# Expert low parts on VectorE, and two output adds per tile instead of one

## The reference

```python
def moe(x, gate_w, expert_w, expert_b):          # _L0_ffn_ref
    xf = x.reshape(B * S, D)
    gate_logits = xf @ gate_w.T
    top_vals, top_idx = jax.lax.top_k(gate_logits, 2)
    w = jax.nn.softmax(top_vals, axis=-1)
    y_all = einsum('td,eod->teo', xf, expert_w) + expert_b[None]
    y_sel = take_along_axis(y_all, top_idx[:, :, None], axis=1)
    return sum(y_sel * w[:, :, None], axis=1)
x = x + attention(layernorm(x), Wq, bq, Wk, bk, Wv, bv, Wo, bo)
x = x + moe(layernorm(x), gate_w, expert_w, expert_b)
```

## Time and profile before

| | |
|---|---|
| median of 3 runs | 1817.34 us (1815.02 to 1827.36) |
| the profiled execution | 1809.88 us, span 1808.1 us |
| TensorE (PE) busy | 1653.4 us, 91% |
| VectorE (DVE) busy | 1432.6 us, 79% |
| ScalarE (ACT) busy | 1272.3 us, 70% |
| GpSimd (POOL) busy | 538.6 us, 30% |

### The profile page before, as it was taken

How to read it: one execution, slowest core, us unless ns; L and a number is a source line. 1 busy time by engine, 2 the same in 40 slices (tenths; PEclk the granted TensorE clock), 3 DMA queues, 4 the chain that set the end, 5 groups by cost and what they waited for, 6 DMA issues and landing times.

```text
span 1808.1 us, 38316 instructions
## 1 busy us (share of the span) xinstructions
PE 1653.4 (91%) x13754; PEld 806.7 (45%) x13755; DVE 1432.6 (79%) x1619; ACT 1272.3 (70%) x2387; POOL 538.6 (30%) x735
## 2 busy tenths in 40 slices
PE   5999999999999999999999999999999987677762
PEld 3533444444444444444444444444444355556551
DVE  3288999999999999999999999999999137653331
ACT  2325888888888888888888888888888953322221
POOL 3111222222233322223223322222224464342222
PEclk9998999999999999999999999999999998688996
DMA  6346422432332243224222332223211433565441
GB/s 195 88 116 138 71 72 58 103 70 58 75 82 60 63 105 82 58 72 102 58 58 60 84 85 64 81 65 67 58 34 37 134 131 134 200 137 99 85 84 20
DMA packets 78946, 155.68 MB, mean 86 GB/s; under 512 B 19504, under 2 KB 23616, under 8 KB 78048
## 3 DMA queue, kind: packets, MB, share of 16 engines
q1 hardware_dynamic: 41776, 72.20, 17.8%
q0 software_dynamic: 34592, 79.71, 16.7%
q10 hardware_dynamic: 2448, 1.84, 0.5%
HBM read 76.38 MB, written 77.67 MB: 85 GB/s over the span
## 4 chain that ended last, share of the span: by engine, by line
PE 79%; DMA 12%; issue 4%; DVE 3%; ACT 1%; ACTq 1%; POOL 1%; SPq 0%; DVEq 0%; POOLq 0%; another core or an unknown queue 0%
PE bank L911 32%; PE bank L872 24%; PE bank L901 16%; DMA out_y<-ys,tok_i 10%; PE bank L844 3%; PE bank L992 1%; DVE max_kc L1166 1%; PE bank L859 1%; DMA x_all<-in_L_attn_x 1%; DMA q_st<-q_parts 0%; DMA arena_p<-in_L_attn_bv 0%; ACTq L662 0%; ACT we_hi L745 0%; PE bank L882 0%; POOL x_all L464 0%
## 5 line engine op out<-in xcount | busy, mean ns | idle before, releaser
L1166 DVE TENSOR_REDUCE max_kc<-bank 128x1 f32<-128x1024 f32 x1024 | 1241.2, 1222 | 75.3 <-PE bank L872 55.3
L735 ACT ACTIVATE arena_p<-bank 128x512 f32<-128x512 f32 x2048 | 1108.7, 596 | 163.4 <-PE bank L901 131.4
L911 PE MATMUL bank<-arena_p,v_cur 128*32 128x256 f32 x8192 | 655.7, 392 | 5.7 <-issue 5.7
L872 PE MATMUL bank<-k_st,q_st 48*128 48x512 f32 x2048 | 511.7, 497 | 5.5 <-DMA q_st<-q_parts 4.2
L901 PE MATMUL bank<-q_st,k_st 50*128 50x512 f32 x2048 | 447.7, 409 | 0.3 <-ACT arena_p L735 0.3
L872 PEld LDWEIGHTS bank<-k_st,q_st 48*128 48x128 f32 x2048 | 191.0, 183 | 430.3 <-issue 384.0
L901 PEld LDWEIGHTS bank<-q_st,k_st 50*128 50x128 f32 x2048 | 298.1, 185 | 35.4 <-ACT arena_p L735 22.4
L911 PEld LDWEIGHTS bank<-arena_p,v_cur 128*32 128x32 f32 x8192 | 162.6, 108 | 292.8 <-issue 149.2
L428 POOL DMA_DIRECT2D sums<-o_acc x128 | 65.3, 516 | 395.9 <-ACT o_acc L715 395.7
L806 ACT ACTIVATE ys<-bank,gate 128x512 f32<-128x512 f32 x39 | 26.8, 687 | 157.8 <-DMA out_y<-ys,tok_i 131.9
L1385 DVE SCALAR_TENSOR_TENSOR ys<-x_all,gate,ys 128x512 f32<-128x512 f32 x39 | 29.3, 751 | 122.9 <-ACT ys L806 120.2
(11 more groups left out here) (161 smaller groups left out, 924.2 us busy)
## 6 DMA issues: line engine op xcount, KB each, us to landing
slots_x<-pad_row POOLq DMA_DIRECT2D x27, 1290.0 KB, 5.8
q_st<-q_parts SPq DMA_DIRECT2D x192, 128.0 KB, 4.6
xs<-slots_x SPq DMA_DIRECT2D x39, 258.0 KB
q_parts<-parts SPq DMA_DIRECT2D x16, 512.0 KB, 3.7
we_raw<-in_L_ffn_expert_w POOLq DMA_DIRECT2D x8, 1024.0 KB, 7.9
at_parts<-o_hl POOLq DMA_DIRECT2D x128, 64.0 KB, 2.3
k_st<-k_parts SPq DMA_DIRECT2D x48, 128.0 KB, 4.8
rec_b<-sums_rec POOLq DMA_DIRECT2D x128, 32.0 KB, 1.9
```

Source lines behind the costliest of these rows:

```text
L735: act.activation(probs[:, u % PRING, :], bank[:, ring_bank(("score", u)), :], ACT.Exp, scale=SCALE).then_inc(p_ready, 1)
L872: return pe.matmul(bank[:, 2 + 2 * (m % 2) + q, :], q_st[r:r + CROW, j % SLOTS, h, qt * P:(qt + 1) * P], k_st[r:r + CROW, key_slot(j // NC ...
L911: mm = pe.matmul(bank[32 * h:32 * h + 32, 6, half], v_cur[:, kt, :], probs[:, (REP * kt + h) % PRING, half], start=(kt == 0 and part == 0) ...
L1166: dve.reduce_max(max_kc[:, m:m + 1], bank[:, 2 + 2 * (m % 2):4 + 2 * (m % 2), :].rearrange("p a s -> p (a s)"), AX.X).then_inc(m_done, 1)
```

## The change

It has two parts. (a) The low parts of experts 0 to 4 are formed on VectorE, each behind the `scaling` of tiles 2, 3, 5, 6 and 9; ScalarE's high part of expert 3 moves from tile 6 to tile 5. (b) Every tile s gets two indirect adds. `add_tile(s, 0)` ("now") is issued with tile s and has the tile's row numbers if the tile ahead has the same expert; otherwise 4096 is added to all of them, so that every row is dropped. `add_tile(s, 1)` ("later") is issued one tile later, behind the "now" add of tile s+1, and has the real numbers exactly where "now" has not. Two tiles of one expert hold no token in common. Before its two adds, step s waits until all "now" adds up to s-2 and all "later" adds up to s-2 have landed; the "now" add of s-1 may be in flight. The flags (`away`) are made with the lists of experts, three small operations in `list_out`, which runs twice.

```diff
+    AWAY = 4096.0
-    POOL_LO = 5
...
-        tok_i = sb("tok_i", [P, TRING, 1], U32)
+        tok_i = sb("tok_i", [P, 2, TRING, 1], U32)
+        away = sb("away", [P, 2, NS])
+        EARLY_SPLIT = (1, 2, 4, 5, 8)
...
+            def add_tile(s, a):
+                pool.indirect_dma_start(out_rows, bass.IndirectOffsetOnAxis(ap=tok_i[:, a, s % TRING, :], axis=0),
+                                        ys[:, s % SR, :], None, bounds_check=T - 1, oob_is_err=False,
+                                        compute_op=ALU.add).then_inc(later_dma if a else now_dma[s % 2], 16)
             def add_rows(s):
                 pool.wait_ge(yb_ready, s + 1)
-                if s > 0:
-                    pool.wait_ge(add_dma, 16 * s)
-                pool.indirect_dma_start(out_rows, bass.IndirectOffsetOnAxis(ap=tok_i[:, s % TRING, :], axis=0),
-                                        ys[:, s % SR, :], None, bounds_check=T - 1, oob_is_err=False,
-                                        compute_op=ALU.add).then_inc(add_dma, 16)
+                if s >= 2:
+                    pool.wait_ge(now_dma[s % 2], 16 * (s // 2))
+                    pool.wait_ge(later_dma, 16 * (s - 1))
+                add_tile(s, 0)
+                if s >= 1:
+                    add_tile(s - 1, 1)
...
-            for e in range(POOL_LO):
-                expert_lo(e)
...
-                if n in (1, 2, 4, 6, 8):
-                    expert_hi(n // 2)
+                if n in EARLY_SPLIT:
+                    expert_hi(EARLY_SPLIT.index(n))
...
-                    act.wait_ge(add_dma, n * 16 - 16 * (SR - 1))
+                    act.wait_ge(later_dma, n * 16 - 16 * (SR - 1))
+                    act.wait_ge(now_dma[ring(s, 2)], halves(s) * 16 - 16 * (SR // 2 - 1))
...
+                link(dve.tensor_tensor(away[:, 0, second], expert_f[:, 0, second], expert_f[:, 0, prior], ALU.not_equal))
+                link(dve.tensor_scalar(away[:, 0, second], away[:, 0, second], AWAY, None, ALU.mult))
+                link(dve.tensor_scalar(away[:, 1, second], away[:, 0, second], -1.0, AWAY, ALU.mult, ALU.add))
...
+                if n - 1 in EARLY_SPLIT:
+                    expert_lo(EARLY_SPLIT.index(n - 1))
...
-                dve.tensor_copy(tok_i[:, ring(s, TRING), :], xs[:, b, TOK:TOK + 1]).then_inc(meta_read, 1)
+                for a in range(2):
+                    ins = dve.tensor_scalar(tok_i[:, a, ring(s, TRING), :], xs[:, b, TOK:TOK + 1], away[:, a, bass.ds(n, 1)],
+                                            None, ALU.add)
+                ins.then_inc(meta_read, 1)
```

More of the change, by code:

```diff
@@ L121, in preln_attention_moe @@
         steps128 = sb("steps128", [P, E, NKT])
-        slot_no = sb("slot_no", [P, NS - S1, E])
+        slot_no = sb("slot_no", [P, NS - S1, 1])
         expert_no = sb("expert_no", [P, 1, E])
@@ L321, in preln_attention_moe @@
         yb_ready = sem("yb_ready")
-        add_dma = sem("add_dma")
+        now_dma = [sem(f"now_dma{b}") for b in range(2)]
+        later_dma = sem("later_dma")
         sp_passed = sem("sp_passed")
@@ L342, in lap, with halves @@
             return s // SR if isinstance(s, int) else s[0] * (UNROLL // SR) + (HEAD + s[1]) // SR
+        def halves(s):
+            return s // 2 if isinstance(s, int) else s[0] * (UNROLL // 2) + (HEAD + s[1]) // 2
         def later(s, d):
@@ L373, in _ @@
                       allow_small_or_imprecise_dtypes=True).then_inc(pool_step, 1)
-            pool.iota(slot_no[:, :, :], [[1, NS - S1], [0, E]], base=0, channel_multiplier=0,
+            pool.iota(slot_no[:, :, :], [[1, NS - S1], [0, 1]], base=0, channel_multiplier=0,
                       allow_small_or_imprecise_dtypes=True).then_inc(pool_step, 1)
@@ L409, in _ @@
             pool.dma_start(bo_sb[:, :], bo.partition_broadcast(P)).then_inc(wc_dma, 16)
-            pool.wait_ge(consts, 6)
+            pool.wait_ge(consts, 8)
             pool.dma_start(wg_sb[:, :, 0:E], gate_w.rearrange("(k p) n -> p k n", p=P)).then_inc(wc_dma, 16)
@@ L492, in _ @@
             divide_outputs(N)
[L494 to L497, removed]
             def scatter(n):
@@ L529, in _ @@
                 add_rows(s)
-            pool.wait_ge(add_dma, 16 * NS)
+            pool.wait_ge(now_dma[(NS - 2) % 2], 16 * ((NS - 2) // 2 + 1))
+            pool.wait_ge(later_dma, 16 * (NS - 1))
+            add_tile(NS - 1, 1)
+            pool.wait_ge(now_dma[(NS - 1) % 2], 16 * ((NS - 1) // 2 + 1))
+            pool.wait_ge(later_dma, 16 * NS)
         @block.sync
@@ L826, in _ @@
             pe.wait_ge(ident_ready, 1)
-            pe.wait_ge(consts, 6)
+            pe.wait_ge(consts, 8)
             def transpose_chunk(c):
@@ L1116, in _ @@
             dve.memset(pad_row[:, :], 0.0).then_inc(consts, 1)
+            dve.memset(away[:, 0, :], 0.0).then_inc(consts, 1)
+            dve.memset(away[:, 1, :], AWAY).then_inc(consts, 1)
             dve.memset(wg_sb[:, :, :], 0.0).then_inc(consts, 1)
-            dve.wait_ge(consts, 3)
+            dve.wait_ge(consts, 5)
             dve.memset(pad_row[:, TOK:TOK + 1], NO_TOKEN).then_inc(consts, 1)
@@ L1289, in experts_of @@
                 link(dve.reduce_sum(tiles_of[:, 3, :], grid8[:, :, :], AX.X))
-                link(dve.tensor_tensor(done_before[:, 0:n, :], tiles_of[:, 3:4, :].to_broadcast(left), slot_no[:, 0:n, :],
-                                       ALU.is_le))
+                link(dve.tensor_tensor(done_before[:, 0:n, :], tiles_of[:, 3:4, :].to_broadcast(left),
+                                       slot_no[:, 0:n, :].to_broadcast(left), ALU.is_le))
                 link(dve.reduce_sum(expert_f[:, 0, first:first + n], done_before[:, 0:n, :], AX.X))
@@ L1307, in list_out @@
                 link(dve.tensor_scalar(expert_rev[:, mine], expert_f[:, 0, mine], -1.0, float(E), ALU.mult, ALU.add))
+                second, prior = slice(max(first, 1), first + n), slice(max(first, 1) - 1, first + n - 1)
+                link(dve.tensor_tensor(away[:, 0, second], expert_f[:, 0, second], expert_f[:, 0, prior], ALU.not_equal))
+                link(dve.tensor_scalar(away[:, 0, second], away[:, 0, second], AWAY, None, ALU.mult))
+                link(dve.tensor_scalar(away[:, 1, second], away[:, 0, second], -1.0, AWAY, ALU.mult, ALU.add))
                 dve.tensor_scalar(expert_i[:, mine], expert_f[:, 0, mine], float(E - 1), None, ALU.min).then_inc(list_ready, 1)
```

## The result

The changed kernel takes 1868.42 us (median of 4 runs, 1866.61 to 1873.75) against 1816.18 us for the kernel before (4 runs, 1810.77 to 1827.36): a ratio of 1.0284, interval 1.0231 to 1.0337, or some 52 us more. The forecast was 1841 us, at most 1855. The sign was right and the size was wrong by more than a factor of two.

A forecast was written before the change was run, and what follows sets the result against it. The prediction took the serial chain of GpSimd's adds to bound the expert stage. Two adds per tile cost 35.5 us and part (a) saves 12: +23.5 on the median 1817.3 gives 1841 us, range 1825 to 1855.

The forecast's parts named there:

- Part (a), 12 us sooner: Output stage: TensorE gets back 15 us, less 2 for VectorE's subtractions and 1 for flags; bounds 4 and 18.
- rival 3: Output stage: VectorE becomes the bound, so the gain is only 4 us, 1849 us in all; chance 0.15.
- rival 2: Output stage: gives back all VectorE lost, 19.4 us less the flags, 1835 us in all; chance 0.13.
- add 0 still at 1581 or later: Sign of a wrong forecast, at the first add of the expert stage, which was expected at about 1573 us.
- A step waits for everything of the step ahead: Expert stage: no step starts before the last "later" add of the step ahead lands; second add starts 1.86 us behind.
- Rivals 1: GpSimd behind the first add: the second add is cheaper, each of 38 steps 0.48 us shorter, 1823 us; chance 0.12.
- 5 (steps that do not wait): Expert stage: GpSimd's two adds and a gap set the pace, about 4.1 us a step, 1751 us; chance 0.02.
- The landing of the second add: Expert stage: time from a second add's start to its landing, taken as 2.70 us empty and 4.93 full.
- the 5.39 of an empty pair: Chain of adds, steps with both adds empty: 1.86 + 2.70 + 0.83 us; 13 such steps, 70.1 us.
- the 7.58 of a real second add: Chain of adds, 13 steps with "later" real: 1.86 + 5.72 us each, 98.5 us; bounds 7.3 and 8.
- the 5.75 of the third kind: Chain of adds, ten steps with "now" real and "later" empty: 57.5 us; bounds 5.39 and 5.8 each.
- Rival 4: Pairs crowd DMA engines beside SyncE's loads, or VectorE stretches GpSimd's operations: 0.25 us per step, 9 us, 1850 us; chance 0.08.

The follow-up runs named there:

- dyn: Kernel before with part (a), one add per tile; a flag from the data branches GpSimd around the wait for the add just ahead; 1748.06 us, ratio 0.9664.
- static: Kernel before with part (a), one add per tile; waits for the add just ahead only at 14 tiles written as constants; 1741.45 us, ratio 0.9627.

## Why the prediction was wrong, point by point

- **What bounds the expert stage: right.** The chain of adds does. With it at 283, 258, 214 or 157 us, the kernel's time moved along.
- **Part (a), 12 us sooner, bounds 4 and 18: right.** 9.6 us in the changed kernel, 10.9 alone; neither the 4 us of rival 3 nor the 18.4 of rival 2. The sign "add 0 still at 1581 or later" did come up, at 1582.56, but only as this execution's stage began 7.3 us late; in the other five kernels with part (a) add 0 is at 1574.72 to 1577.83. The stalls were GpSimd's subtractions: with them away the small operations are short, with them back one takes 13.16 us. The Trainium skill ("SBUF — State Buffer", section "SBUF: two separate sides") has VectorE and GpSimd share a port pair as an exclusive lock, held for a whole instruction; the runs agree. They show besides that an operation that is held up does not always get in between two instructions of the other engine: the 12.38 us of the earlier trace rows began beside the first of three subtractions and ended with the third. The other direction is there as well, and no cost of it can be seen: a GpSimd product that takes 1.28 us as a rule took 2.62 in the changed kernel, beside a subtraction on VectorE of 2.28 (timelines of VectorE and GpSimd).

```profile
1483.19 2.28 DVE L1242 TENSOR_TENSOR we_lo<-we_raw,we_hi 128x2048 fp32r<-128x2048 f32 x1
...
1484.01 2.62 POOL L443 TENSOR_TENSOR o_acc<-o_acc,rec_b 128x512 f32<-128x512 f32 x1 [1.70 <-DMA rec_b<-sums_rec]
```

- **A step waits for everything of the step ahead: right**, and it makes the permission for two "now" adds void. In no step did the next begin before the second add had landed. The second add starts 1.86 us behind the first (1.90 to 2.35 in eight of the 38 steps) and takes GpSimd 1.56 us, empty or not. Rivals 1 (a cheaper second add) and 5 (steps that do not wait) fall.
- **The landing of the second add: this step failed.** The forecast took it from adds that had the DMA engines almost to themselves, 2.70 us empty and 4.93 full, in two places: the 5.39 of an empty pair and the 7.58 of a real second add. A second add starts 1.86 us into the step, and so meets SyncE's load, which a full add of the kernel before was mostly ahead of. The two terms, and the 5.75 of the third kind, came out at 6.59, 9.04 (mean of the ten) and 6.94 us. Steps 5 to 29 took 191.7 us instead of the 159.2 of the forecast; 24 to 25 of these 32.5 go when the load is gone or moved (167.8 and 167.0 us). The empty adds that gave the 2.70 are at the end of the list, where nothing is loaded; I had noted that they were empty, but not that they were alone.
- **What remains, some 8 us of these steps**, is the same term with no load beside it. More than half of it, 4.7 us, is a second thing the forecast left out: in nine of the ten steps with "later" real the add in front is full as well, and the link is 8.10 instead of 7.58, over the upper bound of 8. Where the add in front is empty, as the forecast silently took it, it was right: 7.66 and 7.52 us (step 7 of the kernels without the load and with it moved). The rest is an empty add behind a full one, 5.9 to 6.1 instead of 5.75 (upper bound 5.8), 2.5 us, and 1.3 us in the empty pairs.
- **The other steps.** Steps 30 to 38 took 55.7 us instead of 51.8, of it 2.4 in step 30, which is a pair of empty adds and took 7.79, 6.60, 6.81 and 7.10 us in the four kernels with pairs; that one I didn't follow up. Steps 0 to 4 took 33.3 us instead of the 33.9 of the sum, and the 2 us added for scatters and loads did not show there.
- **Rival 4** had the right place and a price of 9 us for all 38 steps; measured, the load cost 25 us. I gave it 0.08, because in the kernel before the loads cost next to nothing, which the run without them confirms (2 us). It did not follow that they would stay so.
- **The range.** It added the bounds of the two parts, and the top of the chain was +42. That top came from the links' own bounds (8 and 5.8), which were worked out without a load beside the second add, or a full add in front of it.

**What stays open.** Why a second add that meets the load lands about 1 us later. Two explanations fit. Its packets may queue behind the load's bytes in the same DMA engines; or its semaphore is written only behind each engine's earlier writes, as the Trainium skill has it ("DMA: Bandwidth & Descriptors", section "Queues, rings and completion order"). The runs agree with that rule so far as they bear on it: in the four kernels with pairs no step with a full add and an empty one behind it was shorter than the same step of the kernel before, which has the full add alone; the nearest are 5.90 against 5.79 us (step 14, loads moved). But every run that moved or removed the load changed both, so none tells them apart.

## What to carry to other kernels

A DMA's landing time belongs to its place in time as much as to its size: before a duration is taken from a row, look at what else the DMA engines carry at the offset where the new transfer will be, the one issued just ahead of it included, and not only whether that traffic was harmless so far. An operation that a flag turns into nothing still costs its full issue, here 1.56 us on GpSimd and 5.4 us of a serial chain for an empty pair; where an order depends on data, branch around the wait rather than issue a dummy. And where a wait counts a semaphore that the very last instruction ahead will raise, all overlap in front of it is void, whatever the other semaphores allow.

## What the hardware showed that I had not expected

- The same 258 KB load costs a chain of adds 2 us or 25 us, by whether it runs behind the transfer that is waited for or with it. One added wait on SyncE took the chain from 283.4 to 258.3 us and the median from 1868.42 to 1845.23; the ratios to the kernel before, 1.0284 and 1.0207, are closer, since that kernel's own median was 7.5 us lower beside the second.
- Of two full adds 1.86 us apart the second pays. In `dyn` the first of such a pair lands after 4.72 to 5.26 us (adds 9, 12, 15, 18 and 21), in `static` after 4.90 to 5.92; 4.93 was an add alone. So the first is held up little or not at all, and the second more: add 25 of `dyn`, started 1.89 us behind add 24 and with loads beside it, landed after 6.50 us.

```profile
1686.89 6.50 DMA out_y<-ys,tok_i
```

- The flag and the branch on GpSimd are cheap: `dyn`'s chain is 3.2 us longer than `static`'s over 39 tiles, its median 6.6 us.
